# Position attention on one Trainium2 core: which engine makes the products, who normalises the router's rows, and turns written out

## The reference, cut to what matters

```
ln1 = layer_norm(hidden, ln1_weight, ln1_bias)
qkv = ln1 @ qkv_weight.T                   # q: 16 heads, k and v: 4 heads, of 16
score[s, t, h] = sum_d q[s, h, d] * k[t, h // 4, d] / 4      for t <= s
prob = softmax over t
ao[s] = sum_t prob[s, t, h] * v[t, h // 4, :]
h1 = hidden + ao @ proj_weight.T
ln2 = (h1 - mean) / sqrt(var + 1e-5) * ln2_weight + ln2_bias
logits = ln2 @ router_weight               # 8 experts, the best two are taken
```

## Time and profile before

| | us |
|---|---|
| median of three runs | 1906.93 |
| the profiled execution | 1907.43 |
| its span | 1905.60 |
| this stage, from its first product to the next stage's first instruction | 733.2 to 955.1 |

### The profile page before, as it was taken

How to read it: one execution, slowest core, us unless ns; L and a number is a source line. 1 busy time by engine, 2 the same in 40 slices (tenths; PEclk the granted TensorE clock), 3 DMA queues, 4 the chain that set the end, 5 groups by cost and what they waited for, 6 DMA issues and landing times. The chain is left out here.

```text
span 1905.6 us, 32393 instructions
## 1 busy us (share of the span) xinstructions
PE 1668.5 (88%) x10424; PEld 1264.2 (66%) x10424; DVE 1039.7 (55%) x2643; ACT 607.7 (32%) x1768; POOL 501.9 (26%) x638
## 2 busy tenths in 40 slices
PE   4999989999999973677849999996899998799998
PEld 2666667777778642566747888884666666465655
DVE  3444437777777775998651222212788887322221
ACT  1333345555445332122341111111344444211110
POOL 2222220000000035875303332232555542100000
PEclk9999989999999987787868999998999999799999
DMA  8566620000000000000123323332110010000000
GB/s 215 100 100 100 100 45 12 13 12 13 12 12 1 1 9 6 1 23 22 45 95 96 111 90 89 100 84 99 29 34 28 28 33 7 1 22 11 22 11 22
DMA packets 92114, 88.31 MB, mean 46 GB/s; under 512 B 11314, under 2 KB 81906, under 8 KB 91634
## 3 DMA queue, kind: packets, MB, share of 16 engines
q1 hardware_dynamic: 74226, 57.79, 12.7%
q0 software_dynamic: 6912, 18.88, 3.8%
q10 hardware_dynamic: 10880, 10.49, 1.6%
HBM read 46.62 MB, written 23.20 MB: 37 GB/s over the span
## 5 line engine op out<-in xcount | busy, mean ns | idle before, releaser
L794 ACT ACTIVATE probs<-psS,nm 128x256 f32<-128x256 f32 x256 | 118.9, 469 | 182.7 <-DVE nm L827 182.7
L1645 DVE COPY YE<-e_psY 128x512 f32<-128x512 f32 x40 | 27.7, 692 | 220.6 <-PE e_psY L1591 220.6
L1581 PE MATMUL e_psH<-e_XT,w 128*128 128x256 f32 x640 | 146.8, 383 | 0.0
L1591 PE MATMUL e_psY<-w,e_HT 128*128 128x256 f32 x640 | 144.0, 379 | 0.0
L1551 POOL DMA_INDIRECT XE<-token_rows,held x80 | 76.0, 950 | 229.5 <-PE e_psX L1568 179.4
L825 DVE TENSOR_REDUCE mx<-psS 128x2 f32<-128x512 f32 x128 | 87.9, 687 | 83.6 <-PE psS L715 81.2
L715 PE MATMUL psS<-Rec,QT 128*128 128x256 f32 (+1 forms) x512 | 132.4, 382 | 0.9 <-ACT QT L782 0.9
L1591 PEld LDWEIGHTS e_psY<-w,e_HT 128*128 128x128 f32 x640 | 121.8, 190 | 16.3
L1581 PEld LDWEIGHTS e_psH<-e_XT,w 128*128 128x128 f32 x640 | 120.5, 193 | 15.1
L1621 ACT ACTIVATE e_HT<-e_psH 128x512 f32<-128x512 f32 x80 | 47.8, 597 | 233.3 <-PE e_psH L1581 233.3
L446 PE MATMUL psKV<-wkv,XT 128*128 128x512 f32 x256 | 117.4, 602 | 0.0
(11 more groups left out here) (257 smaller groups left out, 3521.1 us busy)
## 6 DMA issues: line engine op xcount, KB each, us to landing
KD<-KV SPq DMA_DIRECT2D x256, 66.0 KB, 2.4
expert_out<-YE ACTq DMA_DIRECT2D x40, 256.0 KB, 2.2
w<-in_w SPq DMA_DIRECT2D x16, 512.0 KB, 4.7
X<-in_x SPq DMA_DIRECT2D x8, 512.0 KB, 7.3
x_turned<-XT SPq DMA_DIRECT2D x32, 128.0 KB, 2.2
XS<-x_turned SPq DMA_DIRECT2D x8, 512.0 KB, 3.9
token_rows<-o_XN SPq DMA_DIRECT2D x32, 128.0 KB, 1.7
out_x<-X SPq DMA_DIRECT2D x8, 512.0 KB, 2.9
```

What stands on the lines that cost most here:

```text
L794: nc.scalar.activation(probs[:, b.q % 4, hg, :], psS[b.q % 2][:, hg, :], ACT.Exp, bias=nm[:, b.q % 2, hg:hg + 1], scale=scale, accum_out=s ...
L1581: mm = pe.matmul(psH[c % 2][half][:, m, :], w1[:, s, kc, f:f + P], XT[:, c % 2, kc, :], start=(m == 0 and kc == 0), stop=(m == 1 and kc == ...
L1591: mm = pe.matmul(psY[c % 2][:, j, :], HT[:, c % 2, m, j * P:(j + 1) * P], w2[:, s, m, :], start=(j == 0 and m == 0), stop=(j == 1 and m == ...
```

## The change

The scores of row 1 and the values of row 2 go from DVE to POOL, so that DVE makes only those of row 7: own products of DVE fall from 10 + 11 to 8 + 8 a block, POOL's rise from 26 + 25 to 28 + 28, in 10 units of each kind instead of 9. The sum over d of row 1 stays on DVE. The places of DVE's own products and of its additions are written anew. `normed` moves from DVE to ACT as an Identity activation with scale `rstd` and bias `shift` = -mean * rstd, for which DVE computes one small `shift` more a block; on ACT it stands at the start of step s, ahead of the copy of row s. The loop over turns 2 and 3 is written out, and the ring buffers run on across turns.

```diff
-    own_rows_s, own_rows_v = (1, 7), (2, 7)
+    own_rows_s, own_rows_v = (S - 1,), (S - 1,)
...
-    assert NU == len(value_units) == 9 and len(own_values) == 3
+    NO = len(own_values)
+    assert NU == len(value_units) == 10 and NO == len(own_scores) == 2
...
-        ownV = k.sb(ctx, "ownV", [P, 3, G, D])
+        ownV = k.sb(ctx, "ownV", [P, NO, G, D])
...
+        shift = k.sb(ctx, "o_shift", [P, S])
+        scaled = k.sem(ctx, "a_scaled")
...
-            with eng.Fori(2, TS) as i:
+            for i in range(2, TS):
                 turn(i, True, True, True)
...
-                            ins = score_product(nc.gpsimd, prodS[:, m % 3, t - t0, :], i, s, t)
+                            ins = score_product(nc.gpsimd, prodS[:, (i * NU + m) % 3, t - t0, :], i, s, t)
...
-                            ins = value_product(nc.gpsimd, prodV[:, n % 3, t - t0, :], i - 1, s, t)
+                            ins = value_product(nc.gpsimd, prodV[:, ((i - 1) * NU + n) % 3, t - t0, :], i - 1, s, t)
...
+            def normed(j, s):
+                act.wait_ge(scaled, j + 1)
+                act.wait_ge(t_ready, j * S + s + 1)
+                act.wait_ge(row_stored[s % 4], j * 32 + (s // 4 * 16 + 16))
+                hs = k.HS[:, bass.ds(j + s * TS, 1), :].rearrange("p a c -> p (a c)")
+                nc.scalar.activation(XN[:, s % 4, :], hs, ACT.Identity, bias=shift[:, s:s + 1],
+                                     scale=rstd[:, s:s + 1]).then_inc(xn_ready, 1)
...
                 for s in range(S + 3):
+                    if last and s < S:
+                        normed(i - 2, s)
                     if leaving and s < S:
...
                 dve.wait_ge(root, j + 1)
+                dve.wait_ge(xn_ready, j * S) if not (isinstance(j, int) and j == 0) else None
                 ch.step(nc.vector.reciprocal(rstd[:, :], var[:, :]))
-
-            def normed(j, s):
-                dve.wait_ge(t_ready, j * S + s + 1)
-                dve.wait_ge(row_stored[s % 4], j * 32 + (s // 4 * 16 + 16))
-                hs = k.HS[:, bass.ds(j + s * TS, 1), :].rearrange("p a c -> p (a c)")
-                nc.vector.tensor_scalar(XN[:, s % 4, :], hs, mean[:, s:s + 1], rstd[:, s:s + 1],
-                                        ALU.subtract, ALU.mult).then_inc(xn_ready, 1)
+                nc.vector.scalar_tensor_tensor(shift[:, :], mean[:, :], -1.0, rstd[:, :], ALU.mult, ALU.mult).then_inc(scaled, 1)
...
-            own_score_at, own_value_at = {0: 0, 2: 1, 4: 2}, {1: 0, 5: 1, 6: 2}
-            add_at = {3: 0, 4: 1, 5: 2, 6: 3, 8: 4}
+            own_score_at, own_value_at = {1: 0, 4: 1}, {2: 0, 6: 1}
+            add_at = {4: 0, 5: 1, 6: 2, 7: 3, 9: 4}
...
-                    if last and n >= 3:
-                        normed(i - 2, n - 3)
-                        if not leaving:
-                            chosen(n - 3)
+                    if last and not leaving and n >= 2:
+                        chosen(n - 2)
...
-                if last:
-                    for s in (S - 2, S - 1):
-                        normed(i - 2, s)
-                        if not leaving:
-                            chosen(s)
```

More of the change, by code:

```diff
@@ L1112, in _ @@
             pe.sem_inc(v_used, 3)
-            pe.sem_inc(own_used, 3)
+            pe.sem_inc(own_used, NO)
             pe.wait_ge(weights, 64)
@@ L1124, in attended @@
                     pe.wait_ge(own_made if own else v_made, j * len(us) + n + 1)
-                    src = ownV[:, n, :, :] if own else prodV[:, n % 3, :, :]
+                    src = ownV[:, n, :, :] if own else prodV[:, (j * NU + n) % 3, :, :]
                     for t in range(t0, t1):
@@ L1183, in turn @@
                         n = sum(s_ <= s for s_, _, _ in (own_values if own else value_units))
-                        act.wait_ge(own_used if own else v_used, j * (3 if own else NU) + n + 3)
+                        act.wait_ge(own_used if own else v_used, j * (NO if own else NU) + n + (NO if own else 3))
                         act.wait_ge(h_ready, j * S + s + 1)
@@ L1226, in own_value @@
                 s, t0, t1 = own_values[n]
-                dve.wait_ge(own_used, j * 3 + n + 1)
+                dve.wait_ge(own_used, j * NO + n + 1)
                 pass_gate(k, dve)
@@ L1273, in chosen @@
                     nc.vector.max_index(k.bidx[:, t, :], k.best[:, t, :], k.LG[:, t // TS, t % TS, :])
-            ENTER, LEAVE, LAST = 10 + 3 + 1, S - 2 + 2, 2 + 6 + 1
-            own_score_at, own_value_at = {0: 0, 2: 1, 4: 2}, {1: 0, 5: 1, 6: 2}
-            add_at = {3: 0, 4: 1, 5: 2, 6: 3, 8: 4}
+            ENTER, LEAVE, LAST = S + NO + 1, S - 2 + 2, 2 + 6 + 1
+            own_score_at, own_value_at = {1: 0, 4: 1}, {2: 0, 6: 1}
+            add_at = {4: 0, 5: 1, 6: 2, 7: 3, 9: 4}
             def turn(i, entering, leaving, last):
@@ L1287, in turn @@
                         dve.wait_ge(s_made, i * NU + n + 1)
-                        summed(prodS[:, n % 3, :, :], s, t0, t1).then_inc(s_summed, 1)
+                        summed(prodS[:, (i * NU + n) % 3, :, :], s, t0, t1).then_inc(s_summed, 1)
                         if n in own_score_at:
@@ L1310, in turn @@
                         dve.wait_ge(v_made, i * NU)
-                        dve.wait_ge(own_made, i * 3)
+                        dve.wait_ge(own_made, i * NO)
                     nc.vector.tensor_tensor(by_t_p, by_t, bc(mx[:, :, :].unsqueeze(3), [P, S, NH, S]),
```

## The result

The changed kernel takes 1913.05 us (median of 8 runs, 1907.93 to 1915.90) against 1907.91 of the kernel before (8 runs, 1905.96 to 1909.81): a ratio of 1.0025, with a 95% interval of 1.0014 to 1.0036, or +2.7 to +6.9 us. It is slower: the interval leaves out 1. The loss is smaller than the 8.6 us of the forecast. Its profiled execution took 1913.22 (span 1911.4).

The account below looks back on a forecast made before the run. The path through POOL's value products, PE and ACT was taken to bound turn 3, nearly turn 2; 0 + 3.0 + (2.1 - 0.4) + (3.75 - 0.4) - 0.7 + 1.2 = +8.6 us, 1915.5 us, range 1901 to 1921 (forecast's own 1908 to 1922).

Parts of the forecast that it names:

- turn 1 loss: Turn 1: without statistics, DVE comes late behind the mark; the turn was to last 44.7 us, +3.0.
- the mark: Point in a turn where the first 4 of POOL's last 13 value products end (row 5's first unit).
- the value path: POOL's value products, PE's row 6, ACT's copy, weight and bias, exponential, probabilities; said to set turn 3, 47.8 us.
- From p to the mark: From the probabilities' end (p), POOL's added products cost 5.1 us a turn; mark at 32.9 instead of 28.3, turns 2 and 3.
- The two waits: POOL's waits after p for DVE's sums in turns 2 and 3: 1.9 and 3.4 us, hardly different from before.
- From the mark to p: Turns 2 and 3: 9.4 us to ACT's copy of row 6, then 4.3 and 4.9, together 18.6 us.
- The terms 4.3 and 4.9: ACT's copy of row 6 to the exponential's end, 4.3 us; from there to the probabilities' end, 4.9 us.
- Turn 4: Root 1.8 us earlier, 1.1 us more ahead of ACT's first copy, POOL's wait for PE mostly gone: -0.7 us.
- Turn 5: Eight normalisations in ACT's chain at 0.52 us add 4.2, waits for PE absorb 3.0: +1.2 us (0 to +5).
- The lock: Rival: two-input DVE instructions or `normed` hold POOL throughout, so each that leaves frees at least 0.407 us; 1903.7 us, chance 0.16.
- DVE as the bound: Rival, turns 1 to 3: POOL follows DVE's sums, so work leaving DVE is gained; -20.4 us, 1886.5, chance 0.10.
- ACT holding PE up: Rival: a normalisation ahead of a copy delays PE's row 2, 4 us in each of turns 2 and 3; 1923.5, chance 0.07.

Follow-up runs that it names:

- the second profile: Profile of the changed kernel run again with no edit: profiled execution 1908.98 us, ratio 1.0035 to the kernel before.
- the later places: Changed kernel with DVE's own row 7 products later (scores after units 4 and 6, values after 3 and 8): 1907.03 us, ratio 1.0001 to the kernel before.
- The copy first alone: Changed kernel with ACT's copy of a row ahead of the same row's normalisation, nothing else: ratio 1.0023 to the kernel before.
- the kernel before, where the mark came 4.7 us earlier: Kernel before with the loop written out and DVE's own products placed later: ratio 0.9989 to the kernel before.
- the version with the lowest median: Kernel before, loop written out, normalisations on ACT behind the copies, DVE's own products placed later: 1902.06 us, ratio 0.9974.

## Why the prediction was right, and where its steps were off

**The total.** It came out within the range because misses of opposite sign met: turns 2 and 3 together came 4.3 us below the forecast (6.1 in the second profile), turn 4 3.0 (1.7) above it, turn 0 1.1 below. That they offset each other in part is luck. What the prediction had right is the sign, the turn 1 loss and the path; one of its own signs of being wrong, row 6 at ACT less than 8 us behind the mark, showed in turn 2 of both profiles and in turn 3 of the second.

**The path.** The prediction said that turns 2 and 3 end on the value path and that DVE's relief would turn into waits. The profile shows it: DVE waits 3.69 us for row 4's projection where it had next to none, and the later places, which change no work at all, bring the mark 3.1 us forward and take 5 to 6 us off. Turn 3 shows it best. Without the stretch from the mark to the copy of row 6, whose length goes with the clock, it is 37.4 us before (47.8 - 10.3) and 40.2 and 40.1 in the two profiles of the change: 2.8 more, which is what the mark moved. PE's clock gave 0.9 and 2.6 of it back.

**From p to the mark.** In turn 1 28.3 was forecast and 27.9 came; in turns 2 and 3 32.9, less 0.4, and 31.1 came. The two waits were forecast at 1.9 and 3.4, 5.3 together; 2.47 and 2.83 came, 5.3 together. What was mis-sized is the price of the products: from POOL's seventh score unit to the mark 18.8 us were reckoned and 840.82 - 822.92 = 17.9 came. I let own products and normalisations beside POOL count 0.13 us each. The last 13 value products, 8.6 us with four own products of row 7 and a normalisation or two beside them, take 7.70 when only the former are moved and 7.55 without both: 0.2 us per own product, little per normalisation.

**From the mark to p.** 18.6 was forecast for turns 2 and 3; 17.2 and 18.5 came, 17.2 and 16.9 in the second profile. The terms 4.3 and 4.9 stood; ACT's copy of row 6 came 7.8 and 9.4 us after the mark (7.8 twice in the second profile) instead of 9.4, by the clock. The step was the mean of 8.6 and 10.3, taken because "PE comes to the mark waiting as before": before, the clock behind the marks of turns 2 and 3 was 0.82 and 0.73, here 1.00 and 0.82 or 1.00. So turns 2 and 3 are +1.7 and +3.35 in the forecast, -1.1 and +0.1 to +1.9 in the runs: these are the steps that made the forecast too high. In turn 1 16.4 was forecast and 17.1 came, by two misses: the subtraction takes 4.27 us instead of 2.1, since it was held here and POOL's product before, and the addition of row 4 starts 4.0 us behind the mark instead of 5.4, with the clock there at 1.00 instead of 0.82. It was DVE's end of the turn, as forecast, and +3.3 us against +3.0; the closeness of the two numbers is in part luck.

**Turn 0** was put at 0 within 1 and is -1.1: POOL's 21 and 13 products run at 0.75 and 0.80 us with a wait of 0.62 between, and the maximum starts at 754.63, 22.3 us after the first product, before 22.2; what is saved is row 1's own scores and sum ahead of the probabilities, which I had priced in turn 2 and forgotten here.

**Turn 4** was forecast at -0.7 and is +1.0 and +2.3: the sign is wrong. The steps are three. Statistics ahead of the own values were to bring the root 1.8 us earlier, from 6.7 us after p. In the second profile they bring it 1.7, in the first only 0.6: beside POOL's value products each of the first five small instructions takes either 0.16 us or about 0.6, in the kernel before too, where the seven took 3.2 us in all. In the first profile of the change all five are long, in the second three, and the seven take 4.3 and 3.2; in turn 5, with POOL standing, each takes 0.16 to 0.18. From the root's start to the first copy 1.1 us more was reckoned; 1.5 came, with `shift` at 0.64 us and a wait of 0.94 on ACT. And from the first copy to the end of the turn it is 31.6 and 31.5 us at 0.91 where the kernel before has 30.3 at 0.95. POOL's wait for PE, which was to go for the most part, is still there in two pieces of 4.45 and 2.54 us, off the path. The copy first alone gives 36.8, which shows the second step; the first is read from the rows, of the first profile, the second, and turn 5 of the first:

```profile
909.62 0.63 DVE L241 TENSOR_TENSOR o_mean<-BST 128x8 f32<-128x8 f32 x1
910.17 0.66 DVE L242 TENSOR_TENSOR o_tmp<-BST 128x8 f32<-128x8 f32 x1
```

```profile
909.74 0.63 DVE L241 TENSOR_TENSOR o_mean<-BST 128x8 f32<-128x8 f32 x1
910.30 0.16 DVE L242 TENSOR_TENSOR o_tmp<-BST 128x8 f32<-128x8 f32 x1
```

```profile
944.35 0.18 DVE L241 TENSOR_TENSOR o_mean<-BST 128x8 f32<-128x8 f32 x1
```

**Turn 5** was forecast at +1.2 and is +1.0. The price of a normalisation on ACT was put at 0.52; the group by form has 0.596, with starts 0.5 us apart:

```profile
L1183 ACT ACTIVATE o_XN<-HS,o_shift,o_rstd 128x256 f32<-128x256 f32 x32 | 18.8, 596 | 2.4 <-DVE o_shift L1269 2.4
```

**The rivals.** The lock as I had put it, 0.407 us back per instruction that leaves, did not come: moving the 8 normalisations gave the last 13 products 0.15 us, and each own product about 0.2. Around the subtraction the trace does show one engine holding the other entirely: POOL's product takes 2.28 us instead of 0.73, or the subtraction takes 4.27 instead of 1.92. The rule of the Trainium skill, page "SBUF — State Buffer", section "Who interferes with whom", fits this: it says that a DVE instruction with two inputs in SBUF contends with a GpSimd instruction that reads SBUF, and that the pair is an exclusive lock. The six long subtractions outlast several products of POOL, which the rule does not tell. The four score products of POOL beside own products take 3.1 to 3.4 us, not the 2.9 plus four whole DVE instructions that full blocking of POOL would give: it is DVE that loses, 0.77 us a product instead of 0.41. DVE as the bound is wrong for the changed kernel. It is right for turn 2 of the kernel before, where the mark came 4.7 us earlier and the turn gained 0.4, and for turn 2 of the version with the lowest median; for turn 1 of the kernel before it is only reckoned (37.8 of 41.7 us on the value path). ACT holding PE up was given 0.07 for turns 2 and 3; it happened, in turn 4.

Left open: what decides whether the subtraction or POOL's product is held, whether a small instruction beside POOL takes 0.16 or 0.6 us, and why the same wait of PE was followed by one clock in one run and by another in the next.

## What to carry to other kernels

Find the wait-by-wait path from one turn's landmark to the next before moving work: a busy engine with its waits elsewhere can be relieved without any gain, and the engine that takes the work may be the one on the path, however idle it looks. When work moves, the order on the relieved engine matters as much as the amount: here a table of four numbers was worth 5 to 6 us, as much as the change cost. What is put in front of the instruction that a third engine waits for, even 0.6 us on an engine that is idle for most of the stage, lengthens the turn; whether it comes out in the total was not clear of noise here. And before a turn of one profile is compared with a turn of another, the stretch behind PE's wait is to be read with its granted clock: it was worth up to 2.8 us of a turn here, as much as the effect looked for.

## What the runs showed of the hardware that was not expected

- A DVE subtraction of 128 x 1024 with both inputs in SBUF took 1.9 us with POOL standing. Beside POOL's score products either the subtraction took 1.9 to 2.5 us and one product of POOL 2.24 to 2.31 instead of 0.73, or the subtraction took 4.27 and ended 1.8 us after POOL's last product, none of which was any longer.
- A DVE instruction of 128 x 8 took 0.16 to 0.18 us with POOL standing and either 0.16 or 0.54 to 0.66 beside POOL's value products. DVE's 128 x 256 products took about 0.77 us beside POOL instead of 0.41, and POOL's grew by about 0.2 per DVE product beside them.
- The changed kernel at the same place, after the same 2.31 us of waiting, was granted a mean TensorE clock of 0.60 of 2.4 GHz over 3 us in one run, a mix of the two levels, and 1.00 in another. It moved a turn of 48 us by 1.8 us, and by this the changed kernel's runs can spread over more (1907.93 to 1915.90) than those before (1905.96 to 1909.81); that this is the cause of the spread was not tested.
